# Channel sums of two layer norms in four column strips of one PSUM bank, their inverse roots on 64 lanes x 512, spread over the lanes by DMA; engine orders drawn up anew

## The chip, the cores and the metric

One core of a Trainium2 chip runs the whole program. The metric is the device time of one execution in microseconds, as the median of the runs taken. The chip's engines each work through a queue of their own, in order: PE (TensorE, matrix products, into PSUM), ACT (ScalarE), DVE (VectorE), POOL (GpSimd) and SP (SyncE, which here only issues DMAs). They meet at semaphores alone.

## The reference, cut to what matters

Input and output are four float32 images, each of 256 channels x 32 x 32 pixels. Four residual blocks follow one another, each on the group-normalised image:

```python
x = x + _L0_conv_ref(_gn(x), ...)   # attention of 8 heads, keys from a strided convolution
x = x + _L1_conv_ref(_gn(x), ...)   # layer norm, four chunks of a selective scan, layer norm, projection
x = x + _L2_conv_ref(_gn(x), ...)   # attention between channels
x = x + _L3_conv_ref(_gn(x), ...)   # weighted max pools of 7 window sizes
```

The two norms that the change touches are both in the second block. They run over the 256 channels of every pixel:

```python
def layernorm(x, g, b):
    mu = x.mean(-1, keepdims=True)
    var = x.var(-1, keepdims=True)
    return (x - mu) * jax.lax.rsqrt(var + EPS) * g + b
xn = layernorm(jnp.transpose(x.reshape(B, C, L), (0, 2, 1)), ln_g, ln_b)
...
xm = layernorm(xm, ln_g, ln_b)
out = xm @ proj_w.T + proj_b
```

## The kernel before, in words

An image is held as two chunks of 128 channels on the 128 lanes, with 1024 pixels in a row, so a sum over channels is a sum over lanes and is done on PE with a matrix of 1/256. The work of an image is cut into streams: F (group norm, queries, keys and values of the first block), A (its attention), C (its output projection proj0, the second block's group norm, its first layer norm and the depthwise convolution xd), B (gate z, scan, output product op, second layer norm, projection proj1), D (third block), and M (fourth block; L for the last two images). In the text C0 is stream C of image 0, B2 stream B of image 2, and so on. Matrix products of one image are laid beside vector work of others.

What sets the order of the work is written out as tables: PE_ORDER, ACT_ORDER, DVE_ORDER and SP_ORDER say for each engine from which stream the next step is taken ("C4" is four steps of C, images in turn), and BANKS_* say which of the eight PSUM banks each product uses. An engine stops at the first instruction whose semaphore is not there, whatever stands behind it.

The first norm of an image (steps sums1, ln_mean1, ln_m21, ln_var1, ln_ln1, ln_rstd1, c1, n1, xn):

- ACT squares the group-normalised image GA0 into PT (sq1, L628).
- PE takes the sums (L1637): for each half of 512 pixels a bank, 64 rows of means of GA0 in lanes 0 to 63, 64 rows of mean squares in lanes 64 to 127. For both halves these are eight products of 128x512, in two column strips of 64. A float32 product stands as two records in the profile.
- ACT copies the means of each half out twice, to lanes 0 to 63 and 64 to 127 (L635), and squares them (L638); DVE subtracts (L1090); ACT takes Ln on 64 lanes x 1024 (L645) and Exp of it twice, for the upper and the lower 64 lanes (L648, L650).
- POOL subtracts the mean from both chunks (c1, L939), DVE multiplies by the inverse root (n1, L1099), ACT scales and writes XNP (xn, L659), which the gate product z (PE L1758) and the convolution xd (PE L1744, 36 products a chunk) read.

The second norm is the same on XM (steps sums2 and so on, without a mean): its inverse root, VAR, is multiplied onto the finished projection proj1 (r2, DVE L1169, then x2, L1173), after which the third block's group norm starts (gn2).

```python
for half in range(2):
    s = take(st, b, f"sums{l}_{half}", dve, f"ln_var{l}" if half else f"ln_var{l}_0")
    for cc in range(CC):
        for lo, of in ((0, src), (64, squares)):
            mm = e.matmul(s[lo:lo + 64, :], mat("mean256")[:, 0:64], of[:, cc, hs(half)], start=(cc == 0), stop=(cc == 1))
```

Other lines that the steps name: L1690 scores of the attention for its row maxima, L1130 their maxima on DVE, L1698 their transpose (mT), L1136 and L1139 the maxima as two halves of float16, which SP carries into QST (L495); L1710 the scores again with the maxima, L607 their Exp on ACT, L1725 the weighted sums in four column strips of 32. L1825 is op, L1616 every projection (proj0, proj1, queries, out). L1516 to L1521 centre the third block's value weights once (w2s, w2m, w2v).

## Time and profile before

| | us |
|---|---|
| median of 3 runs | 782.01 |
| lowest and highest of them | 777.88, 782.92 |
| span of the profiled execution (first to last instruction) | 779.7 |
| PE busy | 664.2 |
| DVE busy | 555.0 |
| ACT busy | 418.3 |
| POOL busy | 34.6 |

The page gives no time of the profiled execution but its span. A span leaves out what lies before the first and behind the last instruction. The busy time of PE is modelled and says that matrix products are in flight. Busy shares are means over a pipeline whose stages have different limits, so what an edit is worth is read stage by stage.

### The profile page before, as it was taken

To read this page: it belongs to the slowest core of one execution; us is meant where nothing else is said; L and a number is where in the kernel's file an instruction comes from. 1 tells how busy PE (TensorE), PEld (TensorE's weight loads), DVE (VectorE), ACT (ScalarE), POOL (GpSimd) and SP (SyncE) were. 2 spreads that over 40 slices of the span, in tenths; PEclk is the share of its full clock that TensorE was granted. 3 is DMA by queue.
4 is the path that set the end of the run, shared out by engine and by line. 5 is a ranking of instruction groups with operands and counts; after the bars stand their busy time and mean duration, and the time that the engine had idled before them with its cause. 6 is when DMAs were issued, how large, how long until landed. Compare 5 with 4: busy or idle time off the path is not lost.

```text
span 779.7 us, 9375 instructions
## 1 busy us (share of the span) xinstructions
PE 664.2 (85%) x3384; PEld 313.0 (40%) x3384; DVE 555.0 (71%) x1057; ACT 418.3 (54%) x703; POOL 34.6 (4%) x26
## 2 busy tenths in 40 slices
PE   4948995798999999899999999997498487898585
PEld 3634343243233454343534542443154153545221
DVE  3567148622848585835999989878998976866695
ACT  0303644649688596446875947756856535402301
POOL 3300002000002000000030000000200000000000
PEclk9968997899999999999999999998798889899799
DMA  7350132001000220001004000020000010000101
GB/s 261 104 137 2 55 78 77 2 1 55 1 1 19 64 76 0 2 1 55 0 2 91 11 1 3 14 95 0 1 1 1 0 55 1 0 1 1 55 0 54
DMA packets 15055, 26.87 MB, mean 34 GB/s; under 512 B 3313, under 2 KB 7057, under 8 KB 14882
## 3 DMA queue, kind: packets, MB, share of 16 engines
q1 hardware_dynamic: 11712, 22.80, 9.7%
q10 hardware_dynamic: 3298, 3.48, 1.5%
q8 instruction: 27, 0.44, 0.2%
q14 instruction: 18, 0.15, 0.1%
HBM read 14.09 MB, written 4.19 MB: 23 GB/s over the span
## 4 chain that ended last, share of the span: by engine, by line
PE 51%; DVE 24%; ACT 15%; issue 6%; SPq 1%; POOL 1%; DMA 1%; ACTq 0%; DVEq 0%; POOLq 0%
PE PSB L1616 11%; PE PSB L1744 6%; PE PSB L1725 5%; PE PSB L1650 3%; PE PSB L1758 3%; PE PSB L1637 3%; DVE PA_ L1459 3%; DVE NEGMAX L1130 3%; PE PSB L2015 3%; DVE HB L1454 3%; PE PSB L1710 2%; PE PSB L1690 2%; PE PSB L1825 2%; PE PSB L1574 1%; SPq L468 1%
## 5 line engine op out<-in xcount | busy, mean ns | idle before, releaser
L1130 DVE TENSOR_REDUCE NEGMAX<-PSB 128x2 f32<-128x512 f32 x128 | 78.6, 680 | 15.0 <-PE PSB L1690 14.7
L607 ACT ACTIVATE PT<-PSB 128x512 f32<-128x512 f32 x128 | 65.7, 604 | 31.1 <-PE PSB L1710 31.0
L2015 PE MATMUL PSB<-PA_,PT 128*128 128x512 f32 x112 | 58.6, 658 | 15.8 <-DVE PA_ L1459 7.0
L1744 PE MATMUL PSB<-XNP,WTAP 64*64 64x512 f32 x576 | 63.4, 591 | 0.0
L1690 PE MATMUL PSB<-KST,QST 96*128 96x256 f16 x256 | 41.7, 310 | 12.6 <-DMA KST<-KL 7.3
L1459 DVE TENSOR_TENSOR PA_<-HB 128x1024 f32<-128x1024 f32 x40 | 48.9, 1223 | 4.8 <-PE PSB L2015 4.0
L1454 DVE TENSOR_TENSOR HB<-PA_ 128x1024 f32<-128x1024 f32 x40 | 51.0, 1274 | 0.6
L671 ACT ACTIVATE U<-PSB 64x512 f32<-64x512 f32 x32 | 26.6, 830 | 31.5 <-PE PSB L1744 30.9
L939 POOL TENSOR_TENSOR GA<-GA,PT 128x1024 f32<-128x1024 f32 x8 | 20.9, 2634 | 497.8 <-ACT PT L635 497.8
L1710 PE MATMUL PSB<-QST,KST 98*128 98x512 f16 x128 | 37.4, 408 | 4.7 <-ACT PT L607 1.8
L2015 PEld LDWEIGHTS PSB<-PA_,PT 128*128 128x128 f32 x112 | 20.8, 202 | 47.7 <-issue 43.5
L1690 PEld LDWEIGHTS PSB<-KST,QST 96*128 96x128 f16 x256 | 24.4, 110 | 32.3 <-ACT PT L607 8.2
L1744 PEld LDWEIGHTS PSB<-XNP,WTAP 64*64 64x64 f32 x576 | 21.3, 133 | 37.8 <-issue 37.7
L1725 PE MATMUL PSB<-PT,VT 128*32 128x512 f32 x256 | 34.0, 603 | 0.6 <-DVE NEGMAX L1130 0.3
L1725 PE MATMUL PSB<-PT,ONES 128*32 128x512 f32 x256 | 33.4, 592 | 0.0
L1650 PE MATMUL PSB<-XF,WDS 128*128 128x256 f32 x128 | 31.6, 406 | 0.2 <-DVE NEGMAX L1130 0.2
L1468 DVE SCALAR_TENSOR_TENSOR ACC<-PA_,COEF,ACC 128x1024 f32<-128x1024 f32 x24 | 30.7, 1281 | 0.3
L1616 PE MATMUL PSB<-GA,WP 128*128 128x512 f32 x64 | 30.0, 605 | 0.0
L1847 PE MATMUL PSB<-SQX 128*128 128x257 f32 x128 | 29.6, 386 | 0.4 <-DVE NEGMAX L1130 0.4
L1616 PE MATMUL PSB<-XF,WQ 128*128 128x512 f32 x64 | 29.7, 600 | 0.1
L1616 PE MATMUL PSB<-XR,BUF 128*128 128x512 f32 x64 | 28.9, 597 | 0.1
L1616 PE MATMUL PSB<-PS,WP 128*128 128x512 f32 x64 | 28.7, 599 | 0.0
(293 smaller groups left out, 1278.0 us busy)
## 6 DMA issues: line engine op xcount, KB each, us to landing
XF<-in_x SPq DMA_DIRECT2D x8, 512.0 KB, 3.9
QST<-QH SPq DMA_DIRECT2D x32, 128.0 KB, 2.7
XR<-in_x SPq DMA_DIRECT2D x4, 1024.0 KB, 5.0
out<-ACC SPq DMA_DIRECT2D x4, 1024.0 KB, 4.0
QST<-QL SPq DMA_DIRECT2D x16, 128.0 KB, 2.4
PS<-in_cw ACTq DMA_DIRECT2D x1, 1152.0 KB
WDS<-in_wds SPq DMA_DIRECT2D x1, 1024.0 KB, 6.9
WP<-in_wp SPq DMA_DIRECT2D x2, 256.0 KB, 7.4
```

The costliest lines, as they stand in the source:

```text
L607: e.activation(PROB[:, 4 * kt + j, :], bank("A", b, f"st{g}_{kt}_{j}")[:, :], ACT.Exp)\
L1130: e.tensor_reduce(NEGMAX[:, h, 2 * j:2 * j + 2], bank("A", b, f"s{h}_{j}")[:, :].rearrange("p (t k) -> p t k", t=2), AX.X, ALU.max, negate ...
L1454: e.tensor_tensor(HB[:, 1:1 + H, :], PA4[:, cc, 1:1 + H, 0:W], PA4[:, cc, 1:1 + H, 2:2 + W], ALU.max)\
L1459: e.tensor_tensor(PA4[:, cc, 1:1 + H, 1:1 + W], HB[:, 0:H, :], HB[:, 2:2 + H, :], ALU.max)\
L1468: e.scalar_tensor_tensor(out=acc, in0=interior(PA_, cc), scalar=COEF[:, cc, k:k + 1], in1=acc, op0=ALU.mult, op1=ALU.add).then_inc(*dve_m. ...
L1616: mm = e.matmul(s[:, :], w(cc), src[:, cc, hs(half)], start=(cc == 0), stop=(cc == CC - 1))
L1650: mm = e.matmul(s[:, m * NK:(m + 1) * NK], WDS[:, cc, n % 4, m * P:(m + 1) * P], src, start=(n == 0), stop=(n == 4 * CC - 1))
L1690: mm = e.matmul(s[:, t * NK:(t + 1) * NK], QST[0:96, h, qt * P:(qt + 1) * P], KST[0:96, h, :], start=True, stop=True)
L1710: e.matmul(s[:, :], KST[0:98, h, kt * P:(kt + 1) * P], QST[0:98, h, hs(g % 2)], start=True, stop=True)\
L1725: mm = e.matmul(bank("A", b, f"pv{g}_0", n)[HD * j:HD * j + HD, :], w, PROB[:, 4 * kt + j, :], start=(kt == 0), stop=(kt == 1))
L1744: mm = e.matmul(banks[gi][64 * half:64 * half + 64, :], WTAP[rows, cc, tap(2 * cc + gi, dy, dx), :], XNP[rows, cc, dy + 16 * half:dy + 16 ...
L2015: mm = e.matmul(bank("L", b, f"acc0_{cc}", half)[:, :], DG[:, cc, k, :], PA4[:, cc, 1 + 16 * half:17 + 16 * half, 1:1 + W], start=(k == 0) ...
```

## The change

- PE: both halves and both kinds of sum go into one bank, in four column strips of 32 rows: means of half 0, means of half 1, mean squares of half 0, mean squares of half 1. There are still eight products of 128x512, and one step sums{l} in place of two.
- ACT: one copy of the means (64 lanes x 512, of both halves; first norm only) and one square, then Ln and one Exp on 64 lanes x 512. Before there were four copies and two squares for the first norm, two squares for the second, and Ln and two Exps on 64 lanes x 1024 for each.
- DVE: one subtraction of 64 lanes x 512 in place of two.
- SP: the result lies with half 0 in lanes 0 to 31 and half 1 in lanes 32 to 63. Two DMAs of 32 rows, each row read four times, write it to all 128 lanes (256 KB each). This is done for the mean and the inverse root of the first norm and the inverse root of the second: 24 DMAs in all. POOL waits for the mean's, DVE for the root's.
- All tables of order and banks are new. In SP's table the C and B steps, which wait for ACT, stand in the one queue with the stacking of queries and keys, the loads and the stores.

```diff
             def sums(b, l, src, ready):
-                for half in range(2):
-                    s = take(st, b, f"sums{l}_{half}", dve, f"ln_var{l}" if half else f"ln_var{l}_0")
-                    for cc in range(CC):
-                        for lo, of in ((0, src), (64, squares)):
-                            mm = e.matmul(s[lo:lo + 64, :], mat("mean256")[:, 0:64], of[:, cc, hs(half)], start=(cc == 0), stop=(cc == 1))
-                    mm.then_inc(*pe.step(f"sums{l}_{half}"))
-                    yield
+                s = take(st, b, f"sums{l}", dve, f"ln_var{l}")
+                for cc in range(CC):
+                    for n, of in enumerate((src, src, squares, squares)):
+                        mm = e.matmul(s[32 * n:32 * n + 32, :], mat("mean256")[:, 0:32], of[:, cc, hs(n % 2)],
+                                      start=(cc == 0), stop=(cc == CC - 1))
+                mm.then_inc(*pe.step(f"sums{l}"))
+                yield
...
+            def spread(dst, src, landed):
+                for half in range(2):
+                    rows = src[32 * half:32 * half + 32, :].unsqueeze(1).broadcast_to([32, 4, HALF])
+                    sp.dma_start(dst[:, hs(half)], rows).then_inc(landed, 16)
+
+            def stream_c(b):
+                sp.wait_ge(*act_c.at(b, "ln_mean1"))
+                spread(MEAN1, SUMS_MEAN, mean_spread)
+                yield
+                sp.wait_ge(*act_c.at(b, "ln_rstd1"))
+                spread(RSTD[1], SUMS_RSTD[1], rstd_spread[1])
+                yield
+
+            def stream_b(b):
+                sp.wait_ge(*act_b.at(b, "ln_rstd2"))
+                spread(RSTD[2], SUMS_RSTD[2], rstd_spread[2])
+                yield
...
-                    if l == 1:
-                        for lo in (0, 64):
-                            e.activation(mean[lo:lo + 64, hs(half)], bank(st, b, f"sums{l}_{half}")[0:64, :], ACT.Copy)\
-                             .then_inc(*act.step(f"ln_mean{l}_{half}_{lo}"))
-                            yield
-                    e.activation(var[0:64, hs(half)], bank(st, b, f"sums{l}_{half}")[0:64, :], ACT.Square).then_inc(*act.step(f"ln_m2{l}_{half}"))
-                    yield
+                if l == 1:
+                    e.activation(SUMS_MEAN, bank(st, b, f"sums{l}")[0:64, :], ACT.Copy).then_inc(*act.step(f"ln_mean{l}"))
+                    yield
+                e.activation(SUMS_RSTD[l], bank(st, b, f"sums{l}")[0:64, :], ACT.Square).then_inc(*act.step(f"ln_m2{l}"))
+                yield
...
-                e.activation(var[0:64, :], var[0:64, :], ACT.Ln, bias=EPS[0:64, 0:1]).then_inc(*act.step(f"ln_ln{l}"))
+                e.activation(SUMS_RSTD[l], SUMS_RSTD[l], ACT.Ln, bias=EPS[0:64, 0:1]).then_inc(*act.step(f"ln_ln{l}"))
                 yield
                 e.wait_ge(*act.at(b, f"ln_ln{l}"))
-                e.activation(var[64:128, :], var[0:64, :], ACT.Exp, scale=-0.5).then_inc(*act.step(f"ln_rstd_high{l}"))
-                yield
-                e.activation(var[0:64, :], var[0:64, :], ACT.Exp, scale=-0.5).then_inc(*act.step(f"ln_rstd{l}"))
+                e.activation(SUMS_RSTD[l], SUMS_RSTD[l], ACT.Exp, scale=-0.5).then_inc(*act.step(f"ln_rstd{l}"))
...
-                e.wait_ge(*act_c.at(b, f"ln_mean{l}_1_64"))
+                e.wait_ge(mean_spread, 32 * b + 32)
...
-F4 A3 F4 A3 F4 A3 F3 A2 M1 A1 M3
+F4 A3 F4 C2 A3 C2 B1 F4 A3 C2 B1 F3 A2 M1 A1 B1 C2 B1 M3
```

How the order moves, at three places. First PE behind the first norm's sums of image 0. XNP,IPZ is the gate product z, QST,KST of 128x512 the scores with maxima, MAT,NEGMAX the transpose of the maxima, XNP,WTAP the convolution. Before:

```order
L1690 MATMUL PSB<-KST,QST 128x256 x12
L1698 MATMUL PSB<-MAT,NEGMAX 32x128
L1758 MATMUL PSB<-XNP,IPZ 64x512 x4
L1710 MATMUL PSB<-QST,KST 128x512 x8
L1690 MATMUL PSB<-KST,QST 128x256 x16
L1609 MATMUL PSB<-MV_F,MAT 128x4
```

and in the change:

```order
L1700 MATMUL PSB<-KST,QST 128x256 x8
L1708 MATMUL PSB<-MAT,NEGMAX 32x128
L1720 MATMUL PSB<-QST,KST 128x512 x8
L1700 MATMUL PSB<-KST,QST 128x256 x16
L1735 MATMUL PSB<-PT,VT 32x512 x4
L1735 MATMUL PSB<-PT,ONES 32x512 x4
L1720 MATMUL PSB<-QST,KST 128x512
L1620 MATMUL PSB<-MV_F,MAT 128x4
L1754 MATMUL PSB<-XNP,WTAP 64x512 x36
L1768 MATMUL PSB<-XNP,IPZ 64x512 x4
```

The gate product left its place between the transpose and the scores and stands behind half of the convolution.

Second, DVE at the same place. GA<-XR is the group norm's output g1, W2M and W2V the centring of the value weights, NEGMAX the maxima, STAT_F statistics for image 2, PT<-PSB,PT the variance, GA<-GA,PT the product n1, ML the lower half of the maxima. Before:

```order
L1040 SCALAR_TENSOR_TENSOR GB_C<-GM_C,GR_C 128x2
L1046 TENSOR_SCALAR GA<-XR,GR_C,GB_C 128x1024 x2
L1130 TENSOR_REDUCE NEGMAX<-PSB 128x2 x11
L1090 TENSOR_TENSOR PT<-PSB,PT 64x512
L1130 TENSOR_REDUCE NEGMAX<-PSB 128x2
L1090 TENSOR_TENSOR PT<-PSB,PT 64x512
L1130 TENSOR_REDUCE NEGMAX<-PSB 128x2 x4
L992 BN_STATS STAT_F<-XF 128x6
L1136 CAST MH<-PSB 32x128
L1099 TENSOR_TENSOR GA<-GA,PT 128x1024 x2
L1139 TENSOR_TENSOR ML<-PSB,MH 32x128
```

and in the change:

```order
L1054 SCALAR_TENSOR_TENSOR GB_C<-GM_C,GR_C 128x2
L1527 TENSOR_REDUCE W2M<-W2V 128x2
L1529 TENSOR_SCALAR W2M<-W2M 128x2
L1532 TENSOR_SCALAR W2V<-W2V,W2M 128x256 x2
L1060 TENSOR_SCALAR GA<-XR,GR_C,GB_C 128x1024 x2
L1141 TENSOR_REDUCE NEGMAX<-PSB 128x2 x9
...
L1141 TENSOR_REDUCE NEGMAX<-PSB 128x2 x3
L1147 CAST MH<-PSB 32x128
L1150 TENSOR_TENSOR ML<-PSB,MH 32x128
```

The four instructions on the value weights came from the start of the program to before g1, and the products n1 no longer stand ahead of ML. In the part left out, four STAT_F instructions and the variance stand between maxima.

Third, PE at the two norms of image 1 (GA and PT: first norm of image 1) and image 0 (PS and SQX, not shown). G,OPW is op, XF,WQ the queries of image 2, XDS and SQD with MAT its key norm. Before:

```order
L1660 MATMUL PSB<-SQD,MAT 128x256 x2
L1616 MATMUL PSB<-XF,WQ 128x512 x2
L1637 MATMUL PSB<-GA,MAT 64x512
L1637 MATMUL PSB<-PT,MAT 64x512
L1637 MATMUL PSB<-GA,MAT 64x512
L1637 MATMUL PSB<-PT,MAT 64x512
L1825 MATMUL PSB<-G,OPW 128x512
```

and in the change:

```order
L1670 MATMUL PSB<-SQD,MAT 128x256 x2
L1835 MATMUL PSB<-G,OPW 128x512
L1646 MATMUL PSB<-GA,MAT 32x512 x2
L1646 MATMUL PSB<-PT,MAT 32x512 x2
L1646 MATMUL PSB<-GA,MAT 32x512 x2
L1646 MATMUL PSB<-PT,MAT 32x512 x2
L1835 MATMUL PSB<-G,OPW 128x512
L1627 MATMUL PSB<-XF,WQ 128x512 x2
```

The first op product moved ahead of the sums, and the query product that stood ahead of them moved behind.

## Rows read from the trace of the kernel before

**Rows 1.** The page: busy us (share of the span) and instructions of each engine.

```profile
PE 664.2 (85%) x3384; PEld 313.0 (40%) x3384; DVE 555.0 (71%) x1057; ACT 418.3 (54%) x703; POOL 34.6 (4%) x26
```

**Rows 2.** Stretches: length, PE, PEld, DVE, ACT, POOL busy, PEclk, DMA share, GB/s.

```profile
215.00:262.00 47.00, 45.75 (x204) 16.89 (x206) 29.97 (x57) 37.00 (x57) 4.69 (x2) 1.00 0.15 35
345.00:412.00 67.00, 67.00 (x335) 30.25 (x338) 54.80 (x109) 46.36 (x72) 6.95 (x2) 1.00 0.09 25
...
412.00:500.00 88.00, 82.86 (x492) 37.12 (x484) 82.30 (x143) 60.20 (x103) 0.00 (x0) 0.98 0.08 17
...
530.00:562.00 32.00, 16.00 (x86) 7.44 (x88) 28.53 (x80) 22.80 (x41) 4.66 (x2) 0.73 0.00 1
```

**Rows 3.** The chain that ended last, its L1637 pieces: start us, us, what.

```profile
124.68 4.57 PE PSB L1637 x16
...
241.81 3.65 PE PSB L1637 x16
...
385.95 7.02 PE PSB L1637 x32
...
518.99 3.61 PE PSB L1637 x16
...
641.78 3.58 PE PSB L1637 x16
```

**Rows 4.** The same chain: a group of eight products in four column strips.

```profile
148.19 1.92 PE PSB L1725 x16
```

**Rows 5.** Single lines: durations in ns min/median/max, starts; L736 as group: busy us, mean ns.

```profile
L638 ACT ACTIVATE PS<-PSB x8: 574/589/592, 244.2 to 645.4; 64x512 f32<-64x512 f32 x8
L645 ACT ACTIVATE PS<-PS,EPS x4: 1132/1144/1148, 248.5 to 646.8; 64x1024 f32<-64x1024 f32 x4
L648 ACT ACTIVATE PS<-PS x4: 1054/1054/1055, 250.2 to 648.0; 64x1024 f32<-64x1024 f32 x4
L1090 DVE TENSOR_TENSOR PS<-PSB,PS x8: 686/693/694, 245.2 to 646.1; 64x512 f32<-64x512 f32 x8
L736 ACT ACTIVATE PS<-PSB,EPS 64x512 f32<-64x512 f32 (+1 forms) x24 | 16.4, 682 | 0.5
```

**Rows 6.** DMA issues of the page: count, KB each, median us to landing.

```profile
QST<-QH SPq DMA_DIRECT2D x32, 128.0 KB, 2.7
XR<-in_x SPq DMA_DIRECT2D x4, 1024.0 KB, 5.0
...
KST<-KL SPq DMA_DIRECT2D x16, 32.0 KB, 1.9
```

**Rows 7.** The chain through the second norm of image 2: start us, us, what.

```profile
522.62 0.60 ACT PS L638
...
527.39 0.70 DVE PS L1169
```

**Rows 8.** Timeline of image 0's first norm [idle before <- what ended it].

```profile
135.11 0.10 PEld L1698 LDWEIGHTS PSB<-MAT,NEGMAX 128*32 128x32 f32 x1 [4.72 <-DVE NEGMAX L1130]
...
138.14 0.27 DVE L1139 TENSOR_TENSOR ML<-PSB,MH 32x128 f16<-32x128 f32 x1
...
139.95 1.98 PE L1758 MATMUL PSB<-XNP,IPZ 64*64 64x512 f32 x8 [4.44 <-ACT XNP L659]
...
141.86 0.13 PEld L1710 LDWEIGHTS PSB<-QST,KST 98*128 98x128 f16 x2 [1.61 <-DMA QST<-ML]
```

**Rows 9.** Single lines on POOL, DVE and ACT: ns min/median/max, first and last start.

```profile
L939 POOL TENSOR_TENSOR GA<-GA,PT x8: 2337/2354/3647, 130.7 to 550.1; 128x1024 f32<-128x1024 f32 x8
...
L1099 DVE TENSOR_TENSOR GA<-GA,PT x8: 1209/1212/1225, 135.9 to 554.1; 128x1024 f32<-128x1024 f32 x8
...
L659 ACT ACTIVATE XNP<-GA,COL x8: 1230/1242/1247, 137.2 to 555.5; 128x1024 f32<-128x1024 f32 x8
```

**Rows 10.** Timeline of the value weights' centring on DVE.

```profile
26.64 0.69 DVE L1516 TENSOR_REDUCE W2M<-W2V 128x2 f32<-128x512 f32 x1 [9.96 <-DMA PS<-in_cw]
...
27.74 1.82 DVE L1521 TENSOR_SCALAR W2V<-W2V,W2M 128x256 f32<-128x256 f32 x2
```

138 lines of the change are left out of this document (68 added, 70 removed), and 6 rows, old and new, of the table BANKS_B.

## The prediction

> **What bounds the kernel now.** I read the page first. PE is in flight for 85% of the span, ahead of DVE (71%) and ACT (54%) [rows 1]. That is a mean, so next came the stretches. From 345 to 412 us PE is busy for all of 67 us, and from 215 to 262 for 45.75 of 47: there the kernel is bound by PE. From 412 to 500 PE (82.9 of 88) and DVE (82.3) are both full. From 530 to 562 PE is busy for half the time while DVE is at 28.5 of 32: there short steps on DVE, ACT and POOL set the pace [rows 2]. The chain of waits says whether the products to be shortened count. It runs through the sums of six norms in five pieces, of 4.57, 3.65, 7.02 (two norms, one behind the other), 3.61 and 3.58 us, together 22.4 us. The first norms of images 1 and 3 are missing from it [rows 3]. The timeline around image 0's first norm shows PE standing three times: before the transpose at 135.11 for DVE's maxima (4.72 us), before the gate product at 139.95 for XNP (4.44 us), and before the scores at 141.86 for the DMA of the maxima (1.61 us) [rows 8].
>
> **PE, part by part.** A norm's sums are eight products in two strips and take 3.6 us at full clock [rows 3]. The same eight products of 128x512 in four strips stand in the trace already, as the attention's weighted sums: 1.92 us [rows 4]. Each norm saves 3.6 - 1.9 = 1.7 us of PE, the eight of them 13.6 us. What that is worth depends on where it lies.
>
> - Images 1 and 2, first norm, and images 0 and 1, second norm, lie where PE hardly stops (215 to 262, 345 to 412). What goes there shortens the path: 4 x 1.7 = 6.8 us.
> - The other four lie where something waits for the norm's result, and there the whole latency counts, not PE's part.
>
> **The latency of the second norm** (images 2 and 3). Before, image 2 went from 518.99 (first sum, rows 3) to 527.39 (first product with the root) [rows 7]: 8.4 us. Now: sums 1.92; square 0.59; subtraction 0.69; Ln on 64x512 0.68, the mean of L736; Exp about 0.6, since a copy of that width takes 0.59 and Exp on 64x1024 takes 1.05 where Ln takes 1.14; four hand-overs of 0.03 [rows 5]. That is 4.6 us. Then the spread, which no row shows. One DMA of 256 KB lies between 1.9 us (32 KB) and 5.0 us (1024 KB); the nearest row, 128 KB out of 32 lanes, is 2.7 [rows 6]. I take 3.4 for one, and 0.6 for the second, which SP issues behind it, so 4.0 us; the ends are 2.5 and 5.6. Sum 8.6 us against 8.4: +0.2 each, +0.4 for two (ends -1.3 and +1.8 each). So a saving of 1.7 us on PE and of 2.5 us on ACT is paid out again to the DMA.
>
> **The first norm.** ACT drops from 6 x 0.59 + 1.14 + 2 x 1.06 = 6.8 to 0.59 + 0.59 + 0.68 + 0.6 = 2.5 us, over all eight norms 27 us; DVE drops 8 x 0.69 = 5.5 us [rows 5]. I count both at nothing: they lie beside PE, and where they don't they are in the latencies. POOL's subtraction starts when the mean is there. Before, that was 6.0 us after image 0's first sum (124.68 [rows 3] to 130.7 [rows 9]), now 1.9 + 0.6 + 4.0 = 6.5 us. POOL then takes 2 x 2.35 us (up to 3.6 for one beside DVE's work), the root is ready meanwhile, and n1 and XNP follow, 1.2 us each [rows 9]. From the sums' end to the second chunk of XNP that is 0.6 + 4.0 + 4.7 + 1.2 + 1.4 = 12 us, up to 14 with a slow POOL. In images 1 and 2 PE has work to lay over it: the sums that follow, two to four query products, and projection proj1 of 7 us, together about 14 to 15 us. Cover suffices, barely. In image 3 there is none (PE busy for 16 of 32 us [rows 2]), and the new DVE order puts two more steps of the pools, each as wide as n1, ahead of the second n1. I take +1.0 for image 3, with ends of -1.5 and +3.
>
> **Image 0 and the moved steps.** The gate product (1.98 us, rows 8) was made while the scores waited for the DMA of the maxima. Now it stands behind half of the convolution, in a stretch without slack: +2.0. In return the lower half of the maxima no longer stands behind two n1 of 1.2 us [rows 8, 9], but ahead of it DVE now has the value weights' centring (26.64 to 29.56, 2.9 us, part of it beside POOL) [rows 10] and four statistics. I take 0.5 us earlier. Net +1.5, and the sums' own 1.7 us vanish in that wait. At the start the centring hid behind PE's convolution, so its leaving gives nothing.
>
> At image 1 the first op product now stands ahead of the sums and the query product behind them. If DVE hasn't finished the gate by then, PE stops where it had work. Against that, 1.25 of PE's idle 47 - 45.75 us in that stretch can close [rows 2]. I take -1.0 for the new orders altogether, ends -5 and +5, as the rows of before can't show them.
>
> **SP.** Waits for ACT now stand in SP's queue ahead of the stacking of images 2 and 3, of max rows and of the stores. Ahead of the scores of images 2 and 3 PE has the convolution and the transposes, some 20 us, so I count nothing; the store of image 1 must wait for image 3's root, and ACT's statistics of image 2's pools for that store. Nothing too, but with less than 2 us in hand.
>
> **Sum.** -6.8 + 0.4 + 1.0 + 1.5 - 1.0 = -4.9 us. The profiled span of 779.7 becomes 774.8. The median of the runs is 782.0, 2.3 above the span, and I carry the difference over: 777.0 us.
>
> **A rule against it.** A spread reads all its 512 KB out of lanes 0 to 63. From 32 to 128 KB, the latter out of 32 lanes, landing grows by 0.8 us per 96 KB; from 128 to 1024 KB, over all lanes, by 2.3 us per 896 KB [rows 6]. The first slope would make 256 KB 3.8 us, the second 3.0; my 3.4 lies between. The Trainium skill (SBUF — State Buffer, "Door 1: The DMA port swizzle") says that lanes 0 to 63 reach only 8 of the 16 DMA ports, of 436 GB/s in all. By that the two DMAs would need an estimated 2.4 us of transfer, at full rate 1.2 us. The landing would come at about 4.4 or 3.1 us in place of my 4.0, and with four exposed latencies the sum would be -3.3 or -8.5 us. No row shows which.
>
> **The rivals.**
>
> - *All of PE's saving counts.* For: the chain passes six of eight sums, and the relief of 27 us on ACT may close the waits that I charge. Against: PE stands idle around image 3's first norm already. 782.0 - 13.6 = 768.4 us.
> - *Nothing is left.* The orders were drawn up for durations that the chip doesn't keep, and PE stops before op, sums or group norms by what it saved: 782 us. For: at image 1 and 2 PE now reaches products whose inputs DVE makes last. Against: before, the same kind of table left PE almost without gaps.
> - *Slower: the spread lands late.* It takes 7 us in place of 4, because source lanes, repeated reads and two transfers in a row add up. Then images 1 and 2 lose their cover, and five places (first norm of images 1, 2, 3, second of 2 and 3) pay 3 us each, less the slack of about 2: +13, so 790 us. It decides from a spread of about 5.2 us, 4.9 us over four latencies. Against: 1024 KB land in 5.0 us [rows 6].
>
> **Chances.** The forecast (777) 0.50, all of the saving 0.24, nothing left 0.12, late spread 0.14. A measurement of this kernel can tell about 1%, that is 774.2 and 789.8 us. Faster by over 1%: 0.22 of the first rival and 0.08 of the forecast's own spread, 0.30. Slower: 0.14. Within: 0.56. The ends of the unknown costs (spread 2.5 to 5.6 over four latencies: -6 to +6; orders -5 to +5) give, taken as independent, about 8 us to either side. The range goes from 766, below the first rival, to 788, just short of the last.
>
> **What would show it.** Right: the sums take 1.9 us a norm; a spread lands 4 us after ACT's root; ln_rstd2 to r2 of image 2 grows from at once to 4 us while the first sum to r2 stays at 8.4; PE stays full from 345 to 412. Wrong: a spread of 3 us or of 6; PE waiting more than 2 us for XNP before the convolution of images 1 or 2; waits over 1 us before op or sums at image 1; SP late with the stacked queries, seen as PE's scores waiting for QST or KST.

## The result, and the profile after

The changed kernel takes 788.43 us in the median of five runs (784.93 to 790.32), the kernel before 779.08 (777.88 to 782.92). The ratio is 1.0098, with a 95% interval of 1.0064 to 1.0132: it is slower by about 7.7 us, where 777.0 were forecast and the range ended at 788. These two medians lie 9.4 us apart; the ratio isn't their quotient, and it is what is compared below. In the sessions of the experiments the kernel before had medians of 781.6 to 783.3. One per cent is 7.8 us.

The page of the changed kernel, its first part [rows 1]:

```profile
PE 647.1 (83%) x3384; PEld 309.5 (40%) x3384; DVE 553.3 (71%) x1049; ACT 392.5 (50%) x675; POOL 35.4 (5%) x26
```

PE has 17 us less to do and ACT 26, as the change promised. The span went up all the same, from 779.7 to 783.1 us, so PE stands still 20 us longer. The stretches that answer to [rows 2], and the one behind them:

```profile
215.00:262.00 47.00, 45.52 (x244) 17.54 (x246) 26.25 (x48) 31.29 (x49) 4.67 (x2) 1.00 0.18 35
345.00:412.00 67.00, 64.32 (x319) 28.43 (x321) 58.53 (x118) 41.80 (x68) 6.88 (x2) 1.00 0.18 40
412.00:500.00 88.00, 79.57 (x442) 36.98 (x435) 80.10 (x135) 58.28 (x99) 0.00 (x0) 0.94 0.11 23
530.00:562.00 32.00, 9.32 (x48) 5.46 (x52) 27.55 (x70) 14.52 (x26) 5.23 (x2) 0.60 0.18 33
562.00:600.00 38.00, 36.83 (x250) 17.80 (x242) 30.09 (x40) 27.39 (x40) 0.00 (x0) 0.94 0.00 1
```

From 345 to 412 PE was busy all the time, now 2.7 us are idle. From 412 to 500 it idles 3.3 us more and its granted clock is 0.94 where it was 0.98. From 530 to 562 it works 9.3 us in place of 16.0, at a clock of 0.60.

The spreads on the page (KB of each transfer, median us from its issue to its landing), beside the stacking copies [rows 6]:

```profile
QST<-QH SPq DMA_DIRECT2D x32, 128.0 KB, 2.4
...
PT<-PT SPq DMA_DIRECT2D x16, 256.0 KB, 4.1
...
PS<-SQX SPq DMA_DIRECT2D x8, 256.0 KB, 4.1
```

A spread is two transfers, and the page times each by itself. From the issue of the first to the landing of the second eleven of the twelve spreads take 4.8 to 5.2 us and one 5.9, the median 4.9.

The chain of waits through image 2's first norm, where before it ran through PE alone (the 7.02 us of sums of [rows 3], and convolution behind projections):

```profile
378.95 1.90 PE PSB L1646 x16
...
380.87 0.59 ACT PT L653
...
382.15 4.23 DMA PT<-PT
...
386.51 4.59 POOL GA L953
...
391.20 3.28 DVE GA L1110
394.48 0.33 DVE SQD L1084
394.81 1.15 DVE GA L1110
...
395.98 1.34 ACT XNP L674 x2
...
397.42 2.76 PE PSB L1754 x21
```

The sums take 1.90 us, as forecast. Then come copy, spread (4.9 us from the copy's end at 381.46 to the landing at 386.38), POOL's subtraction and the product with the root, 16.6 us from the sums' end to the convolution. Two pieces are longer than their own work: the subtraction takes 4.59 us where its median is 2.3 [rows 9], and n1 3.28 where it takes 1.21. They lie beside each other. The kernel before has the same meeting at image 2, but there it is a pooling step on DVE that takes 3.38 us, and n1 never takes over 1.23.

How far each profile is ahead or behind the kernel before's, at starts of the same instruction (us, from the starts in the two timelines; minus is ahead):

| place | before at | after |
|---|---|---|
| PE, last weighted sum of image 1 | 208.3 | -0.4 |
| PE, last convolution product of image 1 | 268.0 | -5.1 |
| PE, first scores with maxima of image 2 | 292.8 | +0.8 |
| PE, last convolution product of image 2 | 419.0 | -6.0 |
| PE, first scores of image 3 | 429.1 | -2.1 |
| DVE, last sum x2 of image 2 (L1173) | 533.5 | 0.0 |
| ACT, XNP of image 3 | 556.6 | +4.4 |
| PE, last convolution product of image 3 | 576.3 | +5.8 |
| PE, last product of the program | 773.4 | +3.4 |

So at the ends of the two convolutions the kernel was ahead by nearly what I had summed for PE (-6.8), in this execution, which is the fastest of its five; between them it was behind, to which the part on where the orders lose it comes back. What is called the end of image 2's scan output below is this last x2, at 533.5 in the kernel before. Eight profiles of kernels that share this order up to there, among the experiments below, stand 0.8 to 4.7 us later at 208 us than this one: the start of image 1 isn't steady from run to run. That is why one pair of profiles can't settle 8 us, and the experiments were all timed in five rounds or more.

### The profile page after: what moved, and what is told of

It reads as the page before. It is cut to its first block, busy times and chain, and to the rows that moved or that the text cites. A ratio compares the mean times of both kernels' runs of the same rounds, so it can differ in the third digit from the quotient of the medians.

```text
span 783.1 us, 9347 instructions
## 1 busy us (share of the span) xinstructions
PE 647.1 (83%) x3384; PEld 309.5 (40%) x3384; DVE 553.3 (71%) x1049; ACT 392.5 (50%) x675; POOL 35.4 (5%) x26
## 3 DMA queue, kind: packets, MB, share of 16 engines
q1 hardware_dynamic: 15168, 29.10, 13.8%
## 4 chain that ended last, share of the span: by engine, by line
PE 60%; DVE 23%; ACT 6%; issue 5%; DMA 2%; SPq 2%; POOL 1%; ACTq 0%; DVEq 0%; POOLq 0%
PE PSB L1627 11%; PE PSB L1754 8%; PE PSB L1735 6%; PE PSB L1660 4%; PE PSB L1768 4%; PE PSB L1857 4%; DVE NEGMAX L1141 3%; PE PSB L1720 3%; DVE PA_ L1470 3%; PE PSB L2025 3%; DVE HB L1465 2%; PE PSB L1700 2%; PE PSB L1800 2%; ACT PT L628 2%; PE PSB L1835 2%
## 5 line engine op out<-in xcount | busy, mean ns | idle before, releaser
L1141 DVE TENSOR_REDUCE NEGMAX<-PSB 128x2 f32<-128x512 f32 x128 | 80.0, 679 | 24.4 <-PE PSB L1700 24.3
L1754 PE MATMUL PSB<-XNP,WTAP 64*64 64x512 f32 x576 | 66.2, 612 | 16.0 <-issue 13.7
L1465 DVE TENSOR_TENSOR HB<-PA_ 128x1024 f32<-128x1024 f32 x40 | 48.8, 1219 | 0.6
L1479 DVE SCALAR_TENSOR_TENSOR ACC<-PA_,COEF,ACC 128x1024 f32<-128x1024 f32 x24 | 32.6, 1360 | 0.4
```

Source lines behind the costliest of these rows:

```text
L1141: e.tensor_reduce(NEGMAX[:, h, 2 * j:2 * j + 2], bank("A", b, f"s{h}_{j}")[:, :].rearrange("p (t k) -> p t k", t=2), AX.X, ALU.max, negate ...
L1465: e.tensor_tensor(HB[:, 1:1 + H, :], PA4[:, cc, 1:1 + H, 0:W], PA4[:, cc, 1:1 + H, 2:2 + W], ALU.max)\
L1754: mm = e.matmul(banks[gi][64 * half:64 * half + 64, :], WTAP[rows, cc, tap(2 * cc + gi, dy, dx), :], XNP[rows, cc, dy + 16 * half:dy + 16 ...
```

## The experiments

Eighteen kernels were run. The ratio is to the kernel before, measured on the same chip in turn. A difference of two ratios carries both intervals, together 3 to 4 us:

| kernel | sums | orders | ratio | 95% interval |
|---|---|---|---|---|
| (changed kernel) | new | new | 1.0098 | 1.0064 to 1.0132 |
| new_sums_old_orders | new | old | 1.0186 | 1.0148 to 1.0223 |
| old_sums_new_orders | old | new | 1.0242 | 1.0207 to 1.0278 |
| old_sums_new_to_263 | old | new to 263 us | 1.0107 | 1.0071 to 1.0142 |
| old_sums_new_to_413 | old | new to 413 us | 1.0129 | 1.0092 to 1.0167 |
| old_sums_new_to_530 | old | new to 530 us | 1.0138 | 1.0098 to 1.0178 |
| new_sums_new_to_413 | new | new to 413 us | 1.0100 | 1.0064 to 1.0136 |
| new_sums_new_to_530 | new | new to 530 us | 1.0049 | 1.0028 to 1.0070 |
| no_spread | new, no spread | new | 1.0073 | 1.0048 to 1.0097 |
| no_spread_first | new, second norms spread | new | 1.0071 | 1.0043 to 1.0099 |
| no_spread_image3 | new, no spread | new, image 3 edited | 1.0062 | 1.0036 to 1.0089 |
| spread_later | new | new | 1.0243 | 1.0207 to 1.0280 |
| sums_twice | new, twice | new | 1.0248 | 1.0208 to 1.0289 |
| n1_first | new | new, edited | 1.0106 | 1.0070 to 1.0142 |
| stack_early | new | new, edited | 1.0101 | 1.0069 to 1.0133 |
| image3_norm | new | new, edited | 1.0094 | 1.0056 to 1.0131 |
| image3_all | new | new, edited | 1.0085 | 1.0055 to 1.0116 |
| z1_wait | new | new, edited | 1.0098 | 1.0066 to 1.0130 |
| three_places | new | new, edited | 1.0110 | 1.0081 to 1.0139 |

The diffs of orders below name the steps; in the tables they are stream letters and counts.

### Sums and orders apart

The change has two halves, and each was put with the other's old partner.

new_sums_old_orders:

```diff
 changed kernel's functions and step tables
-PE_ORDER, ACT_ORDER, DVE_ORDER, BANKS_*: new
+the same of the kernel before, without the steps that are gone
-SP_ORDER: ... M1 A1 B1 C2 B1 M3
+SP_ORDER: ... M1 A1 B1 C2 M1 B1 M2
```

> The four strips of one bank and the spread by transfers, as in the changed kernel, but every engine in the order of the kernel before (an instruction that is gone leaves no gap, the merged one takes the place of the first, the spreads stand in the transfer queue where the changed kernel has them, one store ahead of the last spread). Theory A, the new orders lose the time (order of VectorE at image 3, late stacking of q and k at images 2 and 3): 772 to 777 us, under the kernel before by 2 to 7, since TensorE's sums shrink from about 3.6 to 1.9 us a norm. Rival B, the spread itself loses it, each first norm waiting some 5 us from the copy of the means to the centring: 785 to 790, slower than before by 6 to 11 us.

old_sums_new_orders:

```diff
 functions and step tables of the kernel before
-PE_ORDER, ACT_ORDER, DVE_ORDER, BANKS_*: old
+new ones, with C or B doubled where sums, means, squares,
+variances and roots have more steps, and a second bank a norm
```

> The sums, copies and roots of the kernel before (two banks a norm, no spread), in the orders and banks of the changed kernel, the added instructions directly behind the ones they belong to, and a second bank for each norm that is free there. Theory A (orders): about 788 to 795, slower than before by 9 or more, for the order keeps its loss and TensorE has its 1.7 us a norm back. Rival B (spread): 776 to 782, level with before.

Measured: 1.0186 and 1.0242, medians of 797.4 and 801.6 us: both lie above the ranges of both theories. In the old orders the new sums are 14.5 us slower than the old ones; in the new orders they are 11.2 us faster (1.0242 to 1.0098). Seen the other way, with the work unchanged the new orders lose 18.9 us, and with the new sums they gain 6.9. The halves don't add. One reserve: where the old sums' extra steps stand in the new orders was my choice, each directly behind the one that it belongs to, and no other placing was run.

Where the new sums lose most in the old orders, DVE at image 0's second norm, and PE behind it:

```profile
262.07 0.69 DVE L1179 TENSOR_TENSOR PS<-PSB,PS 128x512 f32<-128x512 f32 x1 [5.64 <-DMA PS<-SQX]
```

```profile
254.56 7.96 PE L1753 MATMUL PSB<-XNP,WTAP 64*64 64x512 f32 x72 [1.25 <-issue]
269.08 0.56 PE L1619 MATMUL PSB<-MV_D,MAT 128*128 128x4 f32 x2 [6.57 <-ACT SQX L564]
269.57 10.43 PE L1753 MATMUL PSB<-XNP,WTAP 64*64 64x512 f32 x72
```

The root's spread (5.26 us on the chain there) reaches DVE at 262.07. The four scaled outputs and their statistics follow, and PE's small statistics product stands between the two halves of image 1's convolution, as it did before. Before, its input was ready when the first half ended; now PE waits 6.57 us, and its next 72 products take 10.43 us where 7.96 is their time at full clock. From the first to the last product of this convolution the profile goes from 2.1 to 11.4 us behind the kernel before, half of the 18.0 that it is behind at its last product. In the new order the same small product waits for nothing: here the new orders do what they are for and lay work over the spread.

### What the spread costs where it stands now

no_spread, no_spread_first (the latter without the B part). Both leave out spreading, and what waited for it reads what lies in the tile:

```diff
-sp.wait_ge(*act_c.at(b, "ln_mean1"))
-spread(MEAN1, SUMS_MEAN, mean_spread)
...
-e.wait_ge(mean_spread, 32 * b + 32)
+e.wait_ge(*act_c.at(b, "ln_mean1"))
-e.wait_ge(rstd_spread[l], 32 * b + 32)
+e.wait_ge(*act_c.at(b, "ln_rstd1"))
...
-e.wait_ge(rstd_spread[2], 32 * b + 32)
+e.wait_ge(*act_b.at(b, "ln_rstd2"))
```

> The changed kernel without its spreading transfers: no spread is issued, and what waited for one to land waits for ScalarE's copy of the means or its root instead and reads what lies in the tile (leaves out the spreading of mean and root over the 128 lanes, for both norms). Theory G, the landing of the spreads is on the chain (4.2 to 5.3 us from issue to landing at each norm, at images 0, 2 and 3 for the first norm): 776 to 780 us, 8 to 12 under the changed kernel. Rival H, the new orders put other work over it, and the loss lies in the orders or in the clock: 786 to 789.

> The same for the first norms alone (leaves out the spreading of their mean and root; the second norms are spread as in the changed kernel). Theory G: most of what no_spread gains, since the chain of waits of the changed kernel has the transfer of a first norm at image 2 and none of a second norm there: 778 to 782. Rival H: 786 to 789. If the second norms carry the loss, this one stays at 786 to 789 and no_spread alone falls.

spread_later:

```diff
 def spread(dst, src, landed):
+    sp.dma_start(DELAY[:, :], MAT[:, 0, 0:64]).then_inc(delayed, 16)
+    sp.wait_ge(delayed, 16 * len(delays))
```

> The changed kernel with every spread's issue held back by one small transfer that has to land first, some 2.5 to 3 us later each (12 spreads, 8 norms). Theory G: about as much again as the landing costs over its length, 3 norms x 2.5 to 3 us = 6 to 9 us, 794 to 798. Rival H (covered by other work): 788 to 790.

Measured: 1.0073, 1.0071 and 1.0243. All twelve spreads together, issue and landing, are worth 2.0 us in the changed kernel (the intervals overlap, so between nothing and about 5). Theory G said 8 to 12 and falls. But held back by one small transfer each they cost 11.3 us more, which is over theory G's range for that run (794 to 798 us; 800.6 measured) as well as over rival H's. The transfer queue of spread_later at image 0's second and image 3's first norm:

```profile
248.78 0.51 SPq L525 DMA_DIRECT2D DELAY<-MAT  x1
250.54 1.19 SPq L529 DMA_DIRECT2D PS<-SQX  x2
...
556.85 0.51 SPq L525 DMA_DIRECT2D DELAY<-MAT  x1
558.61 1.19 SPq L529 DMA_DIRECT2D PT<-PT  x2
560.46 0.62 SPq L525 DMA_DIRECT2D DELAY<-MAT  x1
563.75 1.19 SPq L529 DMA_DIRECT2D PT<-PT  x2
```

The first spread of a norm is 1.8 us late, the root's behind it 3.3. So the new orders cover a spread of 4.9 us nearly whole, and one that comes 1.8 us later or more they don't. My bound for that, 5.2 us, lies between the two; no run tested it. Nor does spread_later delay the spreads alone: SP itself waits, and the copies, loads and stores behind them in its queue with it. What that adds to the 11.3 us no run shows.

### What PE's time is worth

sums_twice:

```diff
-for cc in range(CC):
+for cc in (0, 1, 0, 1):
     for n, of in enumerate((src, src, squares, squares)):
```

> The changed kernel with the matmuls of each norm's sums run twice over (the second pass gives the same sums): TensorE's work is 1.9 us more a norm, 8 x 1.9 = 15 us at full clock, which also makes each sum 1.9 us later. Theory I, TensorE's time counts one for one at the four norms where it had no idle time before (images 1 and 2 first, 0 and 1 second) and on the chain at the ends of the others: 798 to 803. Rival J, TensorE's time is not what bounds the changed kernel, a saved us of it is lost in the next wait: 789 to 794.

Measured: 1.0248, 11.7 us over the changed kernel. In its trace the two passes of one norm, sixteen products, take 3.45 us at full clock (384.87 to 388.32), so the second adds 1.7 us, 13.8 for eight norms. So 85% of a us of PE counts: close to theory I, which had put it at 15 us for full weight. In these orders PE's saving counted, then. The 11.2 us of the pair above agree, though they hold the spread and ACT's relief as well.

### Local repairs that gained nothing

The trace of the changed kernel shows late steps at two places. At image 3's first norm DVE has:

```diff
-ps6 v1_0 acc1_0 n1_0 t2_0 n1_1 p2_0 ps7 ...
+ps6 v1_0 n1_0 n1_1 acc1_0 t2_0 p2_0 ps7 ...
```

(n1_first.) At 413 to 427 us, for image 3's attention, stack_early moves on ScalarE qh1_0 in front of a1, on VectorE ql1_1 and ql1_0 behind n0_1 and kl0, kl1 behind ps1, and the same steps of image 2.

> The changed kernel with two VectorE instructions of image 3 moved: both multiplications of the first norm by its root ahead of the pooling steps acc1 and t2, which stand between the second root and them. Theory C (the place of these two instructions sets the end): xn is ready at 556.5 instead of 561.0 us in the profile, and the time falls by 3 to 4.5 us, to 784 to 785.5. Rival D (the chip's port and the means' late landing hold the centring on GpSimd, 550.0 to 555.3 us, and the end is set elsewhere): less than 1 us off.

> The changed kernel with the high and low halves of q and the low halves of k of images 2 and 3 computed earlier on ScalarE and VectorE, so that their stacking transfers begin some 7 to 10 us earlier and end 3 to 5 us earlier. Theory E (late stacking makes TensorE wait at 421 us and its clock fall to 1.2 GHz at 425 to 433): scores of image 3 start at 422 to 423 instead of 427.1 us, no half-clock stretch there, and 2 to 4 us off the time. Rival F: VectorE is busy for over nine tenths from 412 us on and sets the pace there, so the scores start earlier but the first norm of image 3 does not, and the time stays within 1 us.

Measured: 1.0106 and 1.0101; rivals D and F hold. Each moved what it named. In n1_first the convolution starts 1.3 us earlier in the profile, 2.1 net of the run's later start, and then:

```profile
559.89 10.11 PE L1754 MATMUL PSB<-XNP,WTAP 64*64 64x512 f32 x72 [11.52 <-issue]
569.82 1.05 PE L1768 MATMUL PSB<-XNP,IPZ 64*64 64x512 f32 x8
572.32 1.09 PE L1768 MATMUL PSB<-XNP,IPZ 64*64 64x512 f32 x8 [1.46 <-ACT SQX L767]
...
574.74 9.52 PE L1754 MATMUL PSB<-XNP,WTAP 64*64 64x512 f32 x72
```

PE waits 1.46 us for a bank that ACT's evictions hold, which wait for statistics that DVE makes behind the pooling, and both halves of the convolution run partly at half clock (10.11 and 9.52 us for 7.96, granted clock 0.69 from 555 to 570 us and 0.89 to 585). In stack_early the queries are stacked 9 us earlier and the scores start no earlier, for the projection z1 ahead of them still waits 2.8 us for a bank behind ACT's evictions. So the next round took the step behind as well:

```diff
 image3_norm (VectorE, ScalarE)
-ps6 v1_0 acc1_0 n1_0 t2_0 n1_1 p2_0 ps7 gap1 acc2_0 pm.. t3_0 .. p4_0 pb3
+ps6 ps7 pm.. v1_0 n1_0 pb3 n1_1 acc1_0 t2_0 p2_0 gap1 acc2_0 t3_0 ..
-xn0 xn1 ln_ln3 ln_rstd3
+ln_ln3 ln_rstd3 xn0 xn1
 image3_all: that, and the group norm's gn_var1 gn_b1 g1_0 g1_1
 ahead of the small steps of the other chains
 z1_wait (VectorE)
-ql1_1 acc4_0 t5_0 ql1_0 p5_0 ps0 acc5_0 ps1 .. ps7 pm.. pb3 t6_0 kl0 kl1
+ql1_1 ql1_0 .. acc4_0 t5_0 p5_0 ps0 ps1 ps2 kl0 kl1 ps3 .. ps7 pm.. pb3 acc5_0
 three_places: all of them
```

> The changed kernel with image 3's VectorE order mended at the first norm: the two multiplications by the root stand ahead of the pooling steps, as in n1_first, and the last pool statistic, the merged statistics behind it and their bias, which TensorE's next step waits for over ScalarE's evictions, stand ahead of the pooling steps too; ScalarE has the root of these statistics ahead of the norm's two outputs. Theory K (two late instructions in a row: with the first out of the way, n1_first showed TensorE waiting 1.5 us for the second and half clock again behind it): the gain that n1_first did not give comes now, 4 to 5 us under the changed kernel, 783.5 to 785. Rival L (the stretch is bound by something else yet): 787 to 790.

> The same, and the group norm ahead of it in VectorE's order of the kernel before (its variance, bias and two outputs ahead of the other chains' small steps, and ScalarE's logarithm and root likewise). Theory K: another 1 to 2 us, 782 to 784. Rival L: as image3_norm.

> The changed kernel with the statistics of image 1's last norm, their bias and the low halves of k of image 3 ahead of two pooling steps on VectorE, and the last high and low halves of q of image 3 earlier. Theory M (at 416 to 427 us TensorE's projection z1 waits 2.25 us for a bank that two evictions behind these statistics hold, its clock then falls for some 8 us; stack_early moved the transfers alone and left this wait at 2.8 us): no wait over 1 us there, clock 1.00 at 420 to 435 us, scores of image 3 at 423 to 425, and 3 to 5 us off the time, 783.5 to 785.5. Rival N (what is gained there is lost at the next wait before 530 us, VectorE's): 787 to 789.

> All three edits together. Theories K and M: 7 to 11 us under the changed kernel, 777.5 to 781.5, level with the kernel before or under it. Rivals: as much as the better of the single ones, 783 to 787.

Measured: 1.0094, 1.0085, 1.0098, 1.0110. Theories K and M fall, all four stay within a per mille or two of the changed kernel, and three_places (791.0 us) even stays above its rivals' 783 to 787. A part of the reason can be read in PE's timeline of image3_norm:

```profile
564.43 9.98 PE L1754 MATMUL PSB<-XNP,WTAP 64*64 64x512 f32 x72 [11.92 <-issue]
574.22 1.91 PE L1768 MATMUL PSB<-XNP,IPZ 64*64 64x512 f32 x16
...
577.90 0.57 PE L1792 MATMUL PSB<-HM,SMALL 16*128 16x1 f32 x4 [1.59 <-DVE HM L1195]
578.40 9.65 PE L1754 MATMUL PSB<-XNP,WTAP 64*64 64x512 f32 x72
```

The bank wait is gone. In its place PE waits 1.59 us for HM, the next small step that DVE has behind two more pooling steps, and that wait again costs clock. And of z1_wait at image 2's scan input:

```profile
424.13 1.09 PE L1768 MATMUL PSB<-XNP,IPZ 64*64 64x512 f32 x8 [1.64 <-ACT SQX L767]
...
426.73 0.57 PE L1792 MATMUL PSB<-HM,SMALL 16*128 16x1 f32 x4 [1.33 <-DVE HM L1195]
```

Waits of 2.25 and 0.39 us became 1.64 and 1.33, and the clock was at 0.50 from 430 to 435 us (in the changed kernel from 425 to 430). From image 2's last convolution product to image 3's, the profiles of the changed kernel and of all these variants take 169 to 170 us, the kernel before 157.3. My reading is that whichever step is pulled forward, the steps around it stand where the order wants them for the old moment. One thing these six kernels have in common limits it: they move steps of DVE and ACT, and PE's instructions stand in the same order in all of them.

no_spread_image3 puts image3_norm's edit on no_spread, to see whether spread and order had hidden each other.

> no_spread (no spreading transfers; leaves out the spreading of mean and root) with the edit of image3_norm on VectorE and ScalarE. Theory R, the landing and VectorE's order cover each other at image 3, so that neither edit alone gains there and both together do: the convolution starts 3 to 5 us earlier and the time is 781 to 784. Rival S, image 3's stretch is paced by VectorE's work whatever ends first: 785 to 788, as no_spread.

Measured: 1.0062 against 1.0073, no difference that can be told; rival S. POOL starts at 546.77, right behind the sums, and the convolution still only at 562.35: between the two stand DVE's statistics and pooling steps.

### Where the orders lose it

As no single step was to blame, the orders were cut in time: the new order on every engine up to a step, the old one behind it.

```diff
 PE_ORDER, ACT_ORDER, DVE_ORDER, BANKS_*
+new ones up to the start of the cut step (263, 413: last product of the
+convolution of image 1, image 2; 530: image 2's last scan output)
+then what is left, in the order and banks of the other kernel
```

> The kernel before's instructions, in the orders and banks of old_sums_new_orders up to the convolution that ends image 2's first norm (413 us in the changed kernel's profile), and from there in those of the kernel before. Theory P, the new orders lose their 19 us behind this point (late steps at 413 to 445 and at image 3's first norm, 530 to 582): 780 to 786, within 4 us of before. Rival Q, they lose it evenly, the early part as much as the late one: 788 to 793.

> The same with the change of orders at the end of image 2's scan output (533 us). Theory P: the part from 413 to 530 us shows as the difference to old_sums_new_to_413, 5 to 8 us, and what is left to 801 us belongs to image 3's first norm, 8 to 11 us: 788 to 793. Rival Q: a third of it each, 794 to 796.

> As old_sums_new_to_413, with the change of orders at the last convolution of image 1's first norm (263 us in the changed kernel's profile). The profiles of the kernels with these orders stand 1 to 3 us behind the kernel before there, and 6 to 8 behind at image 2's scores (293 us). Theory T, the stacking of q and k for image 2 and the norms at 377 to 399 us carry the loss of the first 413 us: 782 to 786. Rival U, it is already lost at images 0 and 1: 788 to 792, as old_sums_new_to_413.

> The changed kernel's instructions in its own orders up to the same convolution, and in the order of new_sums_old_orders behind it. Theory P: the changed kernel's loss behind 413 us is some 9 to 10 us in its own order, while new_sums_old_orders lost 5 there, so 783 to 786, 3 to 5 us under the changed kernel. Rival Q, or the spread is badly placed in the old order there: 788 to 792.

> The changed kernel up to the end of image 2's scan output (533 us) and behind it the order of new_sums_old_orders, where VectorE has the norm's products ahead of the pooling. Theory V, image 3's new order costs 8 us by itself with the old sums, and the same with the new: 780 to 784. Rival W, with the spread to wait for, the old order is no better there (new_sums_new_to_413 was level with the changed kernel): 786 to 790.

With the old sums, so with the same work as before: 1.0107, 1.0129, 1.0138, and 1.0242 for the whole. By these totals the new orders lose 8.4 us up to 263, 1.7 from there to 413, 0.7 to 530 (both within the error) and 8.1 behind 530. But a cut has a price of its own, and the profiles show it (us behind the kernel before, each from one execution):

| place (before at) | whole new order | new to 263 | new to 413 | new to 530 |
|---|---|---|---|---|
| last convolution product, image 1 (268.0) | 0.7 | 3.3 | 3.3 | 1.7 |
| first scores with maxima, image 2 (292.8) | 9.0 | 6.7 | 8.7 | 7.6 |
| last convolution product, image 2 (419.0) | 4.3 | 6.8 | 4.1 | 3.0 |
| first scores with maxima, image 3 (444.8) | 9.0 | 8.2 | 10.6 | 8.8 |
| end of image 2's scan output (533.5) | 11.6 | 9.7 | 12.2 | 11.5 |
| end (773.4) | 17.4 | 7.2 | 10.0 | 6.5 |

The kernel that is cut at 263 is 3.3 us behind at its cut and 6.7 a little further on, where one order meets what the other has left late; the one cut at 413 goes from 4.1 to 12.2 in 115 us of the old order. So how the loss before 530, some 11 us of the 18.9, is split between its stretches isn't settled by the totals. These lie in the ranges of rival Q, theory P and rival U for the cuts at 413, 530 and 263, but with the price of the cut in them, and so decide nothing there. The part behind 530 is settled: the whole new order goes from 11.6 to 17.4 there, the one cut at 530 from 11.5 to 6.5, and the timed difference is 8.1 us. Most of it lies at image 3's first norm: at that image's last convolution product (576.3) the one is 19.6 us behind, the other 12.4.

With the new sums the cut at 413 gives 1.0100, level with the changed kernel, so rival Q. The cut at 530 gives 1.0049, 3.8 us under the changed kernel (by the intervals 1 to 7), though not under the kernel before. That is between theory V and rival W. Its profile stands 4.0 us behind the kernel before's at the end of image 2's scan output and 4.0 at the end of the program: the old order of the tail gives nothing away, where the changed kernel's own loses 3.4. PE at image 3's norm there:

```profile
543.10 1.07 PE L1647 MATMUL PSB<-GA,MAT 128*32 128x512 f32 x2
...
548.48 3.65 PE L1846 MATMUL PSB<-MAT,G 128*128 128x128 f32 x16 [1.74 <-DVE SQX L1277]
561.93 3.31 PE L1769 MATMUL PSB<-XNP,IPZ 64*64 64x512 f32 x16 [9.80 <-ACT XNP L675]
...
565.53 7.96 PE L1755 MATMUL PSB<-XNP,WTAP 64*64 64x512 f32 x72
573.42 0.60 PE L1793 MATMUL PSB<-HM,SMALL 16*128 16x1 f32 x4
573.95 7.96 PE L1755 MATMUL PSB<-XNP,WTAP 64*64 64x512 f32 x72
```

and of the changed kernel:

```profile
540.78 1.07 PE L1646 MATMUL PSB<-GA,MAT 128*32 128x512 f32 x2
...
544.92 2.64 PE L1845 MATMUL PSB<-MAT,G 128*128 128x128 f32 x16 [0.50 <-DVE SQX L1276]
561.23 10.72 PE L1754 MATMUL PSB<-XNP,WTAP 64*64 64x512 f32 x72 [13.67 <-issue]
571.77 1.90 PE L1768 MATMUL PSB<-XNP,IPZ 64*64 64x512 f32 x16
```

From the first sum to the first product that reads XNP it is 18.8 us in the one, 20.5 in the other. And the new order puts the convolution first into the stretch where the clock has just fallen, and the small gate products after it; the old one has the gate products first. There the low clock falls on them (3.31 us for 1.9), and both halves of the convolution take 7.96 us; from the first product that reads XNP to the end of the convolution it is 20.0 us, in the changed kernel 21.5, in n1_first 24.4. Four of the six local repairs gave DVE such an order and all six left PE's alone; only the cut at 530, which changes both, gained. So PE's order at image 3 is the rival that they never tested: DVE's, ACT's and PE's orders and the banks change together in this cut, and no run moves PE's alone.

One wait before 263 us is plain, in the changed kernel as in those with the old sums in the new order, and the kernel before doesn't have it:

```profile
181.51 0.61 PE L1700 MATMUL PSB<-KST,QST 96*128 96x256 f16 x4 [0.35 <-DVE NEGMAX L1141]
184.72 0.37 PE L1708 MATMUL PSB<-MAT,NEGMAX 128*32 128x128 f32 x1 [2.60 <-DVE NEGMAX L1141]
184.89 1.91 PE L1720 MATMUL PSB<-QST,KST 98*128 98x512 f16 x4
...
190.21 1.07 PE L1735 MATMUL PSB<-PT,VT 128*32 128x512 f32 x8 [0.97 <-ACT PT L628]
```

before:

```profile
182.89 0.27 PE L1698 MATMUL PSB<-MAT,NEGMAX 128*32 128x128 f32 x1
183.00 0.81 PE L1710 MATMUL PSB<-QST,KST 98*128 98x512 f16 x3
```

The new order makes the last scores of image 1 and then needs their maxima at once. Behind the wait of 2.60 us four products take 1.91 us, where the kernel before has four in 1.04 at 189 us, and the granted clock from 185 to 190 us is 0.70. At the gate's silu (178.2 us before) the changed kernel's profile is 2.0 us ahead, at the scores with maxima behind this wait 1.9 behind. By 208 it has 2.3 of the 3.9 us back. No run took this wait away by itself.

A second place lies behind the cut at 263, between image 1's convolution and image 2's scores. The changed kernel:

```profile
266.91 1.94 PE L1845 MATMUL PSB<-MAT,G 128*128 128x128 f32 x16 [1.23 <-DVE G L1060]
...
270.90 1.09 PE L1768 MATMUL PSB<-XNP,IPZ 64*64 64x512 f32 x8 [0.85 <-ACT U L686]
273.47 3.58 PE L1687 MATMUL PSB<-WV,XDS 128*128 128x256 f32 x8 [1.49 <-ACT G L696]
```

With the old sums in the new order the same three waits are 1.23, 0.88 and 1.46 us; the kernel before has none over 0.39 there. From image 1's last convolution product to image 2's first scores with maxima the new order falls from 0.7 to 9.0 us behind with the old sums, and from 5.1 ahead to 0.8 behind with the new. By image 2's last convolution product 4.7 and 6.7 us of that are back. From there to image 3's scores with maxima it goes the same way, from 4.3 to 9.0 behind and from 6.0 to 0.6 ahead. So how far the new order is ahead depends on the place where it is read: it reaches the convolutions early and the work behind them late.

## Why the prediction was wrong

- **PE, 1.7 us a norm: right.** The sums take 1.90 us, and sums_twice shows that in the new orders 85% of PE's time at all eight norms counts, 11.7 us, more than the 6.8 that I counted at four. The 6.0 us by which the profile was ahead at the end of image 2's convolution don't show those 6.8: 126 us earlier it was 0.8 behind.
- **The spread, 4.0 us: too small, and charged where it hardly counted.** I meant both transfers together, and they take 4.9; 4.1 is one of them, for which I had 3.4. Image 2's second norm went from its first sum at 517.27 to the first product with the root at 526.91 in 9.6 us, not 8.6. But the sum charged the spread whole in four latencies, 16 us, and with no spread at all the time fell by 2.0. With the spread late by 1.8 to 3.3 us it rose by 11.3, close to the 13 of the slower rival.
- **Cover at images 1 and 2 "suffices, barely": right at image 1, not quite at image 2.** At image 1 PE goes from the sums through proj1 into the convolution without a wait. At image 2 it had the 14 us of work that I counted, but from the sums' end to the convolution it was 16.6 us, not 12 to 14, for the spread was longer and POOL and DVE stretched each other's steps. PE stopped for 2.3 us (395.1 to 397.4), by my own mark ("more than 2 us") a sign against me, but a small one.
- **Image 0, +1.5: not confirmed, and the place beside it missed.** At the last convolution product of image 0 this profile is 2.4 us ahead; the eight others with the same order up to there stand between 1.6 ahead and 1.0 behind, so no cost of that size can be read, nor its absence. What I didn't look at is the second group of image 1's scores at 182 us, which the order changes too. It loses 3.9 us, of which 2.3 come back.
- **Image 3, +1.0 (ends -1.5 and +3): too small.** With the pool steps out of n1's way the convolution starts 2.1 us earlier, net, but n1_first gains nothing by it. The whole order behind 530 us costs 8.1 us with the old sums and 3.8 with the new: the statistics, HM and the bank behind them are late too, and PE has the convolution where its clock is low.
- **"I take -1.0 for the new orders altogether": the step that failed, and with it the adding up.** It treats the orders as a small correction to a sum over instructions. With the work unchanged they cost 18.9 us, nearly four times my widest end, and the new sums in them save 11.2. That the difference is the 7.7 us of the result is so by construction. Taken the other way round, the sums, for which the rest of my sum had -3.9, cost 14.5, and the orders give back 6.9. Neither way is the true one. What the pair shows is that the two don't add: each table of orders goes with the work that it was drawn up for, and neither half has a price of its own. Which steps make that so is shown at some places and not as a whole.
- **The rivals.** "Nothing is left" named the mechanism, orders that don't fit what the chip does, and stopped at zero. The late spread named the time, 790, for the wrong reason: it asked for a spread of 7 us. What I lacked was a rival in which the orders alone lose more than the sums save.

What stays open is where before 530 us the new orders lose their other 11 us (with the old sums): waits of PE at 182 us and at 266 to 273 are shown, not weighed, and the cuts there paid for their own seams. Open is also what PE's order at image 3 does by itself. And the start of image 1 moves by up to 5 us between executions of the same instructions. One row goes with it: from 140 to 150 us PE's granted clock was 0.82 in this execution, 0.77 and 0.82 in the two nearest to it at 208 us, and 0.56 and 0.57 in the two latest. What puts it lower there, no row says.

## What to carry to other kernels

Where the orders of all engines are written out, price an edit of the work and an edit of the orders apart: old work in the new orders and new work in the old ones are two runs, and they would have told here what six local repairs did not. When local repairs gain nothing, cut the order in time and let each side have the other kernel's; read the profile at the cut as well as the total, since the seam can cost as much as what is looked for, and at several places, since an order can be ahead at one and behind at the next. And a wait of PE can cost more than its length, where the products behind it run at the lower clock: look for the granted clock behind each new gap, and at which products stand there.

## What the runs showed of the hardware

- A POOL subtraction of 128x1024 beside wide DVE steps takes 4.59 us in place of 2.34, and the DVE step 3.28 in place of 1.21; in the kernel before, at the same image, 3.65 and 3.34 us, and a pooling step 3.38. The times fit taking turns: at image 2 the subtraction is issued at 386.51, DVE's two pooling steps end at 388.89, and the subtraction ends 2.2 us later; n1 begins at 391.20 beside POOL's second one (391.06, 2.33 us) and ends 1.1 us behind it. The Trainium skill (SBUF — State Buffer, "SBUF: two separate sides") says that a GpSimd step and a VectorE step with two inputs from SBUF lock each other out for a whole instruction; the trace agrees. I hadn't priced it. It isn't the width of the DVE step that matters: in image3_norm a DVE product of 128x8, 0.16 us elsewhere, begins at 557.35 and ends 2.31 us later at 559.66, while POOL's two subtractions run from 554.84 to 559.64.
- PE's granted clock was at its lower level (0.50, 1.2 GHz) behind some gaps and not behind others. It was 0.50 from 425 to 430 us behind a gap of 2.25 us at 421.2, and stayed at 1.00 behind one of 2.34 at 395.1. Where it was low, 72 products took up to 10.7 us for 7.96. That can eat a gain whole: in n1_first the convolution started 2.1 us earlier, net, and its second half ended no earlier.
- A spread of two transfers of 256 KB, each out of 32 lanes, is there 4.9 us after its first issue, as late as one transfer of 1024 KB over all lanes (4.9 in this kernel); one of the two takes 4.1 by the median. Of my two estimates from the Trainium skill (SBUF — State Buffer, "Door 1: The DMA port swizzle"), 4.4 us where source lanes limit it and 3.1 at full rate, the first is the nearer, and both are too low.
